# Preparing two stages' weights and first chunks inside the feed-forward loops ahead of them, with the on-chip memory laid out anew

## The chip, the cores and the metric

The kernel runs on one core of one Trainium2 chip. The metric is the device time of one execution in microseconds (us), the median of the runs. TensorE (PE in the profile) multiplies matrices, PEld is its loading of stationary operands, VectorE (DVE), ScalarE (ACT) and GpSimd (POOL) work on elements, and SyncE (SP) issues the DMAs. On-chip memory is 128 partitions wide; the matmul results go to eight banks of 512 numbers per partition (`PS[0]` to `PS[7]`).

## The reference

Six stages follow one another over 8192 rows of 256 numbers (8 sequences of 1024), each reading the layer norm of the running sum `x`:

```python
x = x + 0.5 * L0_ffn(layernorm(x))    # stage S=0: first feed-forward
x = x +       L0_attn(layernorm(x))   # stage S=1: first attention
x = x + 0.5 * L0_ffn(layernorm(x))    # stage S=2
x = x + 0.5 * L1_ffn(layernorm(x))    # stage S=3: second feed-forward
x = x +       L1_attn(layernorm(x))   # stage S=4: second attention
x = x + 0.5 * L1_ffn(layernorm(x))    # stage S=5

# L0_ffn: blocks of 16 numbers quantized to FP4 and back, on activations and weights
def fp4_linear(x, w): return einsum('bsk,nk->bsn', fp4(x), fp4(w))
h = silu(fp4_linear(x, w_gate)) * fp4_linear(x, w_up)     # 704 wide
out = fp4_linear(h, w_down)

# L0_attn: 16 heads of 16, one decaying state per head
qkv = x @ Wqkv.T + b;  k = k / 4;  g = sigmoid(gamma_raw)
state = g * state + outer(v_t, k_t);  y_t = state @ q_t   # over 1024 steps
out = y @ out_w.T + out_b

# L1_ffn: ternary weights
scale = max(mean(abs(w)), 1e-8);  w_t = clip(round(w / scale), -1, 1)
out = gelu(x @ w1_t.T + b1) @ w2_t.T + b2                 # 1024 wide
```

## The kernel before

All of `x` stays on chip as 64 tiles `X[:, n, :]` of 128 rows; four tiles make a chunk, 16 chunks a stage (`NS`), 64 tiles a stage (`NT`). Every engine's program is one list written out by hand and carried out in order; engines wait for one another only by semaphores. Nothing reorders the work, so the order of the lines is the order of the queues.

Each stage needs three things before its first matmul. (1) Its weights and tables. (2) Chunk 0 normalised: VectorE takes the statistics (`stats`, L181), GpSimd makes the factors (`spread`, L200), ScalarE applies them (`norm`, L212) into `XN`. (3) Chunk 0 turned: TensorE transposes `XN` into a bank (`turn_pe`, L231), ScalarE copies the high part to `XTH` (`turn_act`) and VectorE the rest to `XTL` (`low_dve`).

The loops `ffn0_pe`, `ffn0_act`, `ffn0_dve`, `ffn0_pool` run over tile `n` (chunk `i = n // 4`, place in it `j = n % 4`) and are pipelined over several tiles: in its turn `n` TensorE makes the down-product of tile `n-4` (L575), at `j` 2 and 3 a transposition of half of chunk `i+1` (L233), the up-products of tile `n` in three parts (L46 to L48), between them the transposition of tile `n-3` (L590). VectorE's turn holds two halves of the FP4 rounding (L274, L277), the update of `X` (L643), work on the chunks `i+1` and `i+2`, and the product `fH` of tile `n` (L664) with its block scales. Those on chunks stop at the stage's last chunk (`if i + 1 < NS`).

When such a loop ends, `ffn0_end` (L704) makes every engine wait until the stage is over. Then comes the preparation of the next: `attn0_set_sp`, `_act`, `_dve`, `_pe`, `_pool` for the first attention (weights split in a high and a low part, powers of the decay made on VectorE, written to HBM and read back in shifted form as `hankel`, two matmuls with `rev` at L829 and L830 and their copies to `DT` and `KD`), `ffn1_set_sp`, `_dve`, `_pe` for the second feed-forward (mean of the absolute weights, then the ternary masks at L1185 and L1187, 2048 numbers at a time for each of two matrices). `attn0_ready` and `ffn1_ready` are the waits on it. After them every engine prepares chunk 0 of the stage, and only then comes the first projection (L46) or up-product (L1312). Memory is shared: the attention's buffers start where those of stage 0's loop do, and the buffers of the second feed-forward and attention start at the address of all that came before them.

## Time and profile before

| | us |
|---|---|
| median of 3 runs (2841.96 to 2848.13) | 2843.5 |
| the profiled execution | 2847.05 |
| its span, first to last instruction | 2844.9 |
| TensorE busy | 2573.6 (90%) |
| VectorE busy | 1784.6 (63%) |
| ScalarE busy | 1374.1 (48%) |
| GpSimd busy | 1141.7 (40%) |

The busy shares are averages over stages that differ. A stretch in which TensorE is busy for the whole of its length is bound by TensorE; one in which it stands still shows in its idle time, written in square brackets in a timeline, with the engine or the DMA that ended it. The granted clock is 1.00 at 2.4 GHz and 0.50 at 1.2 GHz. L-numbers are lines of the kernel before.

### The profile page before, as it was taken

To read this page: it belongs to the slowest core of one execution; us is meant where nothing else is said; L and a number is where in the kernel's file an instruction comes from. 1 tells how busy PE (TensorE), PEld (TensorE's weight loads), DVE (VectorE), ACT (ScalarE), POOL (GpSimd) and SP (SyncE) were. 2 spreads that over 40 slices of the span, in tenths; PEclk is the share of its full clock that TensorE was granted. 3 is DMA by queue.
4 is the path that set the end of the run, shared out by engine and by line. 5 is a ranking of instruction groups with operands and counts; after the bars stand their busy time and mean duration, and the time that the engine had idled before them with its cause. 6 is when DMAs were issued, how large, how long until landed. Compare 5 with 4: busy or idle time off the path is not lost.

```text
span 2844.9 us, 75949 instructions
## 1 busy us (share of the span) xinstructions
PE 2573.6 (90%) x31466; PEld 2155.5 (76%) x31466; DVE 1784.6 (63%) x4172; ACT 1374.1 (48%) x2283; POOL 1141.7 (40%) x1382
## 2 busy tenths in 40 slices
PE   4999999678989969999999499989999999979998
PEld 3888888567777757888887388877788888858887
DVE  7878887445555548788785466554556666545554
ACT  3444444234444424444443477765445444417776
POOL 5555555233333325555553233311444444353332
PEclk8999999889999989999999799999999999979999
DMA  4000000100001100000000100000000000000001
GB/s 151 1 1 1 1 1 1 25 13 22 21 21 22 22 16 1 1 1 1 1 1 1 47 1 1 1 5 18 18 17 17 16 18 16 19 3 23 31 30 38
DMA packets 67557, 45.85 MB, mean 16 GB/s; under 512 B 13184, under 2 KB 66192, under 8 KB 67216
## 3 DMA queue, kind: packets, MB, share of 16 engines
q1 hardware_dynamic: 67216, 41.00, 5.2%
q8 instruction: 251, 4.11, 0.6%
q14 instruction: 90, 0.74, 0.1%
HBM read 15.78 MB, written 8.40 MB: 9 GB/s over the span
## 4 chain that ended last, share of the span: by engine, by line
PE 27%; issue 13%; POOL 11%; DVE 6%; ACT 6%; DMA 0%; SPq 0%; POOLq 0%; ACTq 0%; DVEq 0%
PE ps L575 6%; PE ps L46 3%; PE ps L48 3%; PE ps L47 3%; ACT XN L221 2%; PE ps L233 2%; PE ps L1312 2%; POOL rs L206 2%; DVE st L190 2%; POOL a1pry L1887 2%; POOL a1pry L1889 2%; PE ps L1313 2%; ACT gHf L1353 2%; POOL a1l L1875 2%; DVE XTL L243 1%
## 5 line engine op out<-in xcount | busy, mean ns | idle before, releaser
L575 PE MATMUL ps<-WDT,fHT 128*128 128x256 f32 (+1 forms) x1536 | 379.7, 389 | 8.5 <-ACT fHT L615 8.5
L1382 DVE TENSOR_TENSOR gHl<-gHf,gHh 128x512 fp32r<-128x512 f32 x256 | 180.6, 706 | 254.3 <-ACT gHh L1357 254.2
L575 PEld LDWEIGHTS ps<-WDT,fHT 128*128 128x128 f32 (+1 forms) x1536 | 279.3, 190 | 80.1 <-issue 42.5
L687 POOL TENSOR_TENSOR fV<-fH,frc 128x704 f32<-128x704 f32 x128 | 178.3, 1393 | 356.9 <-DVE frc L676 356.9
L46 PE MATMUL ps<-WGH,XTH 128*128 128x512 f32 (+1 forms) x768 | 314.1, 409 | 3.2 <-DVE XTL L243 1.4
L48 PE MATMUL ps<-WGL,XTH 128*128 128x512 f32 (+1 forms) x768 | 290.2, 378 | 0.0
L47 PE MATMUL ps<-WGH,XTL 128*128 128x512 f32 (+1 forms) x768 | 290.0, 378 | 0.0
L1327 PE MATMUL ps<-W2T,gHh 128*128 128x256 f32 x1024 | 256.1, 283 | 0.0
L1329 PE MATMUL ps<-W2T,gHl 128*128 128x256 f32 x1024 | 253.7, 281 | 0.0
L221 ACT ACTIVATE XN<-X,nb,rs 128x256 f32<-128x256 f32 x384 | 198.9, 589 | 98.3 <-POOL nb L210 98.3
L664 DVE TENSOR_TENSOR fH<-ps,fSG 128x704 f32<-128x704 f32 x128 | 113.9, 890 | 194.6 <-ACT fSG L621 183.2
L609 ACT ACTIVATE ps<-fV 128x704 fp32r<-128x704 f32 x128 | 97.5, 762 | 281.2 <-DVE fV L277 273.5
L1312 PE MATMUL ps<-XTH,W1T 128*128 128x512 f32 x512 | 208.8, 408 | 19.6 <-DVE XTL L243 18.3
L1353 ACT ACTIVATE gHf<-ps,B 128x512 f32<-128x512 f32 x256 | 175.2, 684 | 99.8 <-PE ps L1313 99.7
L239 ACT ACTIVATE XTH<-ps 128x512 fp32r<-128x512 f32 x192 | 108.0, 594 | 215.4 <-PE ps L233 215.3
L694 POOL TENSOR_TENSOR fHX<-fV,fsc 128x704 f32<-128x704 f32 x128 | 178.2, 1392 | 69.9 <-DVE fV L277 69.9
L1313 PE MATMUL ps<-XTL,W1T 128*128 128x512 f32 x512 | 204.9, 400 | 0.0
L204 POOL TENSOR_SCALAR ve<-mv 128x4 f32<-128x4 f32 x96 | 32.9, 342 | 426.3 <-DVE mv L196 422.5
L1329 PEld LDWEIGHTS ps<-W2T,gHl 128*128 128x128 f32 x1024 | 193.5, 189 | 10.2
L1327 PEld LDWEIGHTS ps<-W2T,gHh 128*128 128x128 f32 x1024 | 192.8, 188 | 9.6
L1875 POOL TENSOR_TENSOR a1l<-a1l,a1rc 128x128 f32<-128x128 f32 x128 | 49.7, 410 | 363.0 <-DVE a1rc L1842 363.0
L46 PEld LDWEIGHTS ps<-WGH,XTH 128*128 128x128 f32 x768 | 146.4, 191 | 42.5 <-issue 21.2
(227 smaller groups left out, 6395.8 us busy)
## 6 DMA issues: line engine op xcount, KB each, us to landing
X<-in_x SPq DMA_DIRECT2D x16, 512.0 KB, 8.9
a0vp<-a0vt SPq DMA_DIRECT2D x256, 32.0 KB, 1.9
a1vp<-a1vk SPq DMA_DIRECT2D x256, 32.0 KB, 2.2
out<-X SPq DMA_DIRECT2D x16, 512.0 KB, 2.9
tws<-in_w SPq DMA_DIRECT2D x2, 1024.0 KB, 7.8
WN<-in_wgu SPq DMA_DIRECT2D x3, 384.0 KB, 5.0
a0km<-in_wqkv SPq DMA_DIRECT2D x2, 384.0 KB, 3.4
a1pry<-in_aw SPq DMA_DIRECT2D x1, 768.0 KB, 4.5
```

The source lines that it names most:

```text
L46: e.matmul(o, hh, mh, start=first, stop=False)
L47: e.matmul(o, hl, mh, start=False, stop=False)
L48: return e.matmul(o, hh, ml, start=False, stop=last)
L221: t = act.activation(XN[:, j, :], X[:, 4 * i + j, :], ACT.Identity, scale=rs[b][:, j:j + 1], bias=nb[b][:, j:j + 1])
L575: h = pe.matmul(down, HT[n % 2][0:m, c, :], WDT[0:m, c, :], start=(c == 0), stop=(c == 5))
L687: pool.tensor_tensor(s3(V[(n - 1) % 2][:, :]), s3(H[(n - 1) % 2][:, :]), cast16(rc[(n - 1) % 2][:, :], 44), ALU.mult).then_inc(s_hv, 1)
L1312: pe.matmul(PS[m % 2][:, :], W1T[:, k, fs], XTH[b][:, k, :], start=(k == 0), stop=False)
L1313: t = pe.matmul(PS[m % 2][:, :], W1T[:, k, fs], XTL[b][:, k, :], start=False, stop=(k == 1))
L1327: pe.matmul(o, Hh[w][:, js], W2T[:, f, :], start=(f == 0 and j % 2 == 0), stop=False, skip_group_check=True)
L1329: t = pe.matmul(o, Hl[w][:, js], W2T[:, f, :], start=False, stop=(f == 7), skip_group_check=True)
L1353: act.activation(Hf[u][:, :], PS[m % 2][:, :], ACT.Gelu, bias=B1[:, f:f + 1]).then_inc(s_ge, 1)
L1382: dve.tensor_tensor(Hl[m % 8][:, :], Hf[m % 4][:, :], Hh[m % 8][:, :].bitcast(F32), ALU.subtract).then_inc(s_hl, 1)
```

## The change

The preparation of the first attention moves into the loop of stage 0, and that of the second feed-forward into the loop of stage 2. `attn0_set_dve` becomes eight steps at the turns `n` = 10 to 17 of stage 0, `ffn1_set_dve` nineteen steps at the turns 8 to 17, 22, 24 to 31 and 33 of stage 2. `attn0_set_act` runs at turns 8, 9, 34 and 38 and `attn0_set_pe` at 34 and 38 of stage 0, `ffn1_set_pe` at 22 of stage 2. These products use the bank `PS[3]`, which also holds the turned chunks, so TensorE waits there until the bank has been read: `pe.wait_ge(s_dte, n + 1)` and `pe.wait_ge(s_tern, 4)`. The two exponentials of the preparation stand in front of stage 0's loop, and the DMAs of the tables behind those of `x` in SP's list. The DMAs of the ternary matrices are issued when the first attention has ended.

The loop no longer stops at the last chunk: statistics, factors, normalisation, transposition and both copies of the next stage's chunk 0 are done in its last turns. `ffn0_end` goes; `ffn0_banks` and later waits on the last update of `X` stand where banks or memory are reused. In the attention, VectorE takes chunk 1's statistics first. For all this the preparation needs memory of its own: the second half's weights start at 15960 numbers per partition behind the shared tiles, and the masks are made 512 numbers at a time.

```diff
-        lay1 = top.enter_context(ExitStack())
-        W1T = sb(lay1, "W1T", [P, 2, FF], R32)
-        W2T = sb(lay1, "W2T", [P, 8, D], R32)
...
+        sb(lay1, "over", [P, 15960])
+        W1T = sb(lay1, "W1T", [P, 2, FF], R32)
...
         def x_turn_pe(pe, S, i, k):
             F = 16 * S + i
-            pe.wait_ge(s_qxx, 8 * S + i + 1)
+            if i < NS:
+                pe.wait_ge(s_qxx, 8 * S + i + 1)
+            else:
+                pe.wait_ge(s_xn, F + 1)
             if F or k:
                 pe.wait_ge(s_xl, 2 * F + k)
-            turn_pe(pe, F, k, PS[3], XV)
+            turn_pe(pe, F, k, PS[3], XV if i < NS else xf)
...
                     h.then_inc(s_dn, 1)
-                if n < NT and j in (2, 3) and i + 1 < NS:
+                if n == 34 and S == 0:
+                    pe.wait_ge(s_qxx, i + 2)
+                    attn0_set_pe(pe, 0)
+                if n == 38 and S == 0:
+                    pe.wait_ge(s_qxx, i + 2)
+                    attn0_set_pe(pe, 1)
+                if n == 22 and S == 2:
+                    pe.wait_ge(s_qxx, 16 + i + 2)
+                    ffn1_set_pe(pe)
+                if n < NT and j in (2, 3):
                     x_turn_pe(pe, S, i + 1, j - 2)
                 if n < NT:
                     if j == 0:
...
                 t = tb + n
                 i, j = n // 4, n % 4
-                if n < NT and j in (2, 3) and i + 1 < NS:
+                if n in (34, 38) and S == 0:
+                    attn0_set_act(act, 2 + (n - 34) // 4)
...
+                if n == NT - 4:
+                    norm(act, S + 1, 0)
+                if n in (8, 9) and S == 0:
+                    attn0_set_act(act, n - 8)
...
+                if n in when0 and S == 0:
+                    attn0_set_dve(dve, when0.index(n))
+                if n in when1 and S == 2:
+                    ffn1_set_dve(dve, when1.index(n))
+                if n < NT and j < 2 and i + 1 < NS:
+                    x_grid(dve, S, i + 1, j)
+                if n < NT and j > 1:
+                    x_low(dve, S, i + 1, j - 2)
+                if n < NT and j < 3 and i + 2 <= NS:
+                    for k in ((0, 1), (2, 3), (4, 5, 6, 7))[j]:
+                        stats(dve, *chunk(16 * S + i + 2), k)
...
-        def ffn0_end(e, S):
-
-            e.wait_ge(s_dn, 32 * S + NT)
-            e.wait_ge(s_he, 32 * S + NT)
-            e.wait_ge(s_hx, 32 * S + NT)
-            e.wait_ge(s_xd, 64 * S + NT)
...
+        def ffn0_banks(pe, S):
+
+            pe.wait_ge(s_hm, 32 * S + NT)
+            pe.wait_ge(s_hq2, 32 * S + NT)
...
         def attn0_set_sp(sp):
...
-            ffn0_end(sp, 0)
-            for k in range(2):
-                sp.dma_start(KM[k][:, :, :].rearrange("p k t -> p (k t)")[:, 0:768],
-                             wqkv[128 * k:128 * k + 128, :]).then_inc(d_wqkv, 16)
...
+            sp.wait_ge(s_wt, 12)
+            for k in range(2):
+                sp.dma_start(KM[0][:, k, 0:768], wqkv[128 * k:128 * k + 128, :]).then_inc(d_wqkv, 16)
...
+        def attn0_set_exp(act):
+            act.wait_ge(d_gam, 16)
             act.activation(g1[:, 1:2], g1[:, 0:1], ACT.Exp, scale=-1.0).then_inc(s_ga, 1)
...
+        def attn0_set_act(act, n):
+
+            if n < 2:
+                act.wait_ge(d_wqkv, 32)
+                act.activation(a0WH[:, n, :], KM[0][:, n, 0:768], ACT.Copy).then_inc(s_a0h, 1)
...
+        def attn0_set_dve(dve, n):
+
+            if n < 2:
+                dve.wait_ge(s_a0h, n + 1)
+                dve.tensor_tensor(a0WL[:, n, :], KM[0][:, n, 0:768], a0WH[:, n, :].bitcast(F32),
+                                  ALU.subtract).then_inc(s_a0l, 1)
...
+        def attn0_set_pe(pe, n):
+
             pe.wait_ge(d_hank, 96)
-            pe.wait_ge(d_a0, 96)
-            pe.matmul(PS[0][:, :], rev[:, :], hankel[:, 0:512], start=True, stop=True).then_inc(s_dt, 1)
-            pe.matmul(PS[1][:, 0:64], rev[:, :], hankel[:, 512:576], start=True, stop=True).then_inc(s_dt, 1)
+            pe.wait_ge(d_a0, 80)
+            src = hankel[:, 0:512] if n == 0 else hankel[:, 512:576]
+            pe.matmul(PS[3][:, 0:512 if n == 0 else 64], rev[:, :], src, start=True, stop=True).then_inc(s_dt, 1)
...
         def attn0_set_pool(pool):
-            ffn0_end(pool, 0)
...
@@ -946,7 +989,7 @@
                             if k == 1 and q == 3:
                                 t.then_inc(s_up, 1)
 
-            turn_x(0)
+            ffn0_banks(pe, 0)
             proj(0, (0, 1))
...
+                    pe.wait_ge(s_xd, NT)
                 if 0 <= m < NT:
...
-            norm(act, 1, 0)
-            turn_x(0)
             proj(0, (0, 1))
             proj(0, (2, 3))
             norm(act, 1, 1)
+            act.wait_ge(s_dn, NT)
...
-            low(0)
+                stats(dve, 1, 1, k)
             late(0)
-            for k in range(8):
-                stats(dve, 1, 1, k)
...
-            ffn0_end(sp, 2)
...
+        def ffn1_set_dve(dve, step):
+
+            if step < 8:
+                n, c = divmod(step, 4)
+                if c == 0:
+                    dve.wait_ge(d_w[n], 16)
+                t = dve.tensor_reduce(tam[n][:, 16 * c:16 * c + 16],
+                                      tws[n][:, 512 * c:512 * c + 512].rearrange("p (a b) -> p a b", b=32), AX, ALU.add,
+                                      apply_absolute_value=True)
+                if c == 3:
...
+                n, c = divmod(step - 10, 4)
+                cs = slice(512 * c, 512 * c + 512)
+                v, a = tws[n][:, cs], ta[c % 2]
+                dst = (W1T, W2T)[n][:, :, :].rearrange("p k n -> p (k n)")[:, cs]
+                dve.wait_ge(s_tern, 5 + 2 * (step - 10))
+                dve.tensor_scalar(a[:, :], v, ta1[n][:, 3:4], None, ALU.is_lt).then_inc(s_tern, 1)
+                dve.wait_ge(s_tern, 6 + 2 * (step - 10))
+                dve.scalar_tensor_tensor(out=dst, in0=v, scalar=ta1[n][:, 2:3], in1=a[:, :], op0=ALU.is_gt,
                                          op1=ALU.subtract).then_inc(s_tern, 1)
-            dve.wait_ge(d_b1, 32)
...
         def ffn1_set_pe(pe):
-            ffn0_end(pe, 2)
-            for n in range(2):
-                pe.wait_ge(s_tern, 6 * n + 2)
-                pe.matmul(PS[n][:, 0:1], ones[:, :], ta1[n][:, 0:1], start=True, stop=True).then_inc(s_ternp, 1)
+
+            pe.wait_ge(s_tern, 3)
...
         def ffn1_ready(e):
 
-            e.wait_ge(s_tern, 13)
+            e.wait_ge(s_tern, 22)
...
             if S == 3:
-                turn_x(0)
+                ffn0_banks(pe, 2)
             for m in range(8 * NS + LAG):
                 i, f = m // 8, m % 8
+                if S == 3 and m == LAG:
+                    pe.wait_ge(s_xd, 64 * 2 + NT)
...
             if S == 3:
-                norm(act, 3, 0)
-                turn_x(0)
+                act.wait_ge(s_dn, 64 + NT)
...
-            if S == 3:
-                for k in range(8):
-                    stats(dve, 3, 0, k)
-                low(0)
...
+            attn0_set_exp(act)
             ffn0_act(act, 0)
-            attn0_set_act(act)
             attn0_ready(act)
...
             ffn1_act(act, 3)
...
             start_dve(dve)
             ffn0_dve(dve, 0)
-            attn0_set_dve(dve)
             attn0_ready(dve)
...
             ffn1_ready(dve)
...
```

TensorE's list where the first attention opens (L575/L591 down-products, L590/L615 transpositions of the last tiles, a0wh the attention's weights), before:

```order
L590 MATMUL ps<-ident,fHX 64x128
L575 MATMUL ps<-WDT,fHT 128x256 x6
L829 MATMUL ps<-a0qp,a0rev 128x512
L830 MATMUL ps<-a0qp,a0rev 128x64
L233 MATMUL ps<-ident,XN 128x128 x8
L46 MATMUL ps<-XTH,a0wh 128x512
```

and now:

```order
L591 MATMUL ps<-WDT,fHT 128x256 x6
L615 MATMUL ps<-ident,fHX 128x128 x5
L615 MATMUL ps<-ident,fHX 64x128
L591 MATMUL ps<-WDT,fHT 128x256 x6
L46 MATMUL ps<-XTH,a0wh 128x512
```

The two products with `a0rev` and the eight transpositions of `XN` no longer stand between the last down-product and the first projection.

TensorE's list at the start of turn 34 of the first stage (the rows end with the turned chunk's transposition and the first up-products), before:

```order
L47 MATMUL ps<-WGH,XTL 128x384
L48 MATMUL ps<-WGL,XTH 128x384
L575 MATMUL ps<-WDT,fHT 128x256 x6
L233 MATMUL ps<-ident,fXV 128x128 x4
L46 MATMUL ps<-WGH,XTH 128x512
```

and now:

```order
L47 MATMUL ps<-WGH,XTL 128x384
L48 MATMUL ps<-WGL,XTH 128x384
L591 MATMUL ps<-WDT,fHT 128x256 x6
L871 MATMUL ps<-a0qp,a0rev 128x512
L246 MATMUL ps<-ident,fXV 128x128 x4
L46 MATMUL ps<-WGH,XTH 128x512
```

One product with `a0rev` has come in between the down-product and the transpositions; its 64-column fellow stands in the same place four turns later.

ScalarE's list in front of stage 0's loop (fXV the chunk's FP4 values, a0g and a1g the two tables of exponentials), before:

```order
L480 ACTIVATE WDT<-ps 64x256
L309 ACTIVATE ps<-fXV 128x512
L621 ACT_TABLE_LOAD
L621 ACTIVATE fSG<-ps 128x704
L309 ACTIVATE ps<-fXV 128x512
```

and now:

```order
L496 ACTIVATE WDT<-ps 64x256
L322 ACTIVATE ps<-fXV 128x512
L813 ACTIVATE a0g<-a0g 16x1
L815 ACTIVATE a1g<-a1g 128x16
L648 ACT_TABLE_LOAD
L648 ACTIVATE fSG<-ps 128x704
```

The exponentials have come in front of the table load; the load that stood before them in the first gap and the one at the opening of stage 2 are gone from ScalarE's list.

## Rows read from the trace of the kernel before

**Rows 1.** The page: granted clock of TensorE, tenths of full speed, 40 slices of 71.1 us.

```profile
PEclk8999999889999989999999799999999999979999
```

**Rows 2.** Stretches around both stage changes: length, engines' busy us, clock, DMA share, GB/s.

```profile
495.00:530.00 35.00, 35.00 (x172) 28.48 (x170) 19.46 (x38) 10.99 (x15) 12.16 (x9) 1.00 0.00 1
530.00:549.50 19.50, 13.92 (x56) 9.53 (x56) 4.87 (x10) 3.11 (x4) 4.16 (x3) 0.91 0.00 0
549.50:581.60 32.10, 4.30 (x12) 2.74 (x12) 7.93 (x31) 7.10 (x13) 5.71 (x12) 0.58 0.24 55
1553.00:1570.50 17.50, 11.93 (x56) 8.16 (x54) 4.50 (x9) 3.11 (x4) 4.16 (x3) 1.00 0.00 0
1570.50:1603.50 33.00, 3.09 (x13) 2.58 (x13) 16.71 (x26) 4.03 (x7) 6.48 (x24) 0.57 0.32 102
```

**Rows 3.** Timeline of TensorE at the first change: start, us, engine, line [idle<-releaser].

```profile
546.37 3.05 PE L575 MATMUL ps<-WDT,fHT 128*128 128x256 f32 x12 [0.90 <-ACT fHT L615]
568.56 2.04 PE L829 MATMUL ps<-a0qp,a0rev 128*128 128x512 f32 x2 [19.14 <-DMA a0GQ<-pw_scratch]
570.40 0.53 PE L830 MATMUL ps<-a0qp,a0rev 128*128 128x64 f32 x2
...
581.66 0.80 PE L46 MATMUL ps<-XTH,a0wh 128*128 128x512 f32 x1 [1.41 <-DVE XTL L243]
```

**Rows 4.** Timeline of the other engines in the first gap.

```profile
555.36 1.83 DVE L800 TENSOR_TENSOR a0wl<-a0km,a0wh 128x768 fp32r<-128x768 f32 x2 [5.48 <-ACT a0wh L786]
...
570.96 0.60 ACT L793 ACTIVATE a0DT<-ps 128x512 f32<-128x512 f32 x1 [13.38 <-PE ps L830]
```

**Rows 5.** Timeline of TensorE at the second change.

```profile
1567.39 3.05 PE L575 MATMUL ps<-WDT,fHT 128*128 128x256 f32 x12 [0.90 <-ACT fHT L615]
...
1603.50 0.79 PE L1312 MATMUL ps<-XTH,W1T 128*128 128x512 f32 x1 [1.41 <-DVE XTL L243]
```

**Rows 6.** Timeline of VectorE in the second gap.

```profile
1582.34 1.29 DVE L1185 TENSOR_SCALAR ta<-tws,ta 128x2048 f32<-128x2048 f32 x1
1583.66 2.35 DVE L1187 SCALAR_TENSOR_TENSOR W1T<-tws,ta 128x2048 fp32r<-128x2048 f32 x1
```

**Rows 7.** Timeline of TensorE inside the first feed-forward loop, tiles two to four.

```profile
152.57 2.95 PE L575 MATMUL ps<-WDT,fHT 128*128 128x256 f32 x12
...
160.44 2.95 PE L575 MATMUL ps<-WDT,fHT 128*128 128x256 f32 x12
...
167.90 2.95 PE L575 MATMUL ps<-WDT,fHT 128*128 128x256 f32 x12
```

**Rows 8.** VectorE's waits from 90 to 520 us: us in total, times, longest.

```profile
DVE fH L664 <- ACT fSG L621: 81.1, 54, 3.1
```

**Rows 9.** Timeline of VectorE inside the same loop.

```profile
156.33 0.88 DVE L277 SCALAR_TENSOR_TENSOR fV<-ps,fV 128x704 f32<-128x704 f32 x1
...
160.69 0.89 DVE L664 TENSOR_TENSOR fH<-ps,fSG 128x704 f32<-128x704 f32 x1 [0.70 <-ACT fSG L621]
```

**Rows 10.** Timeline of the DMA issues and ScalarE at the start.

```profile
6.03 20.94 SPq L259 DMA_DIRECT2D X<-in_x  x15
...
43.80 1.28 ACT L621 ACT_TABLE_LOAD   x1
48.82 0.76 ACT L621 ACTIVATE fSG<-ps 128x704 f32<-128x704 f32 x1 [3.74 <-PE ps L48]
```

**Rows 11.** Short stretches that open the first attention and the second feed-forward kind.

```profile
581.60:590.00 8.40, 8.01 (x30) 6.46 (x30) 3.19 (x11) 3.74 (x6) 0.35 (x2) 0.79 0.00 0
1603.50:1610.00 6.50, 6.50 (x17) 5.06 (x18) 2.96 (x10) 4.10 (x7) 0.50 (x1) 0.57 0.00 0
```

**Rows 12.** Timeline of ScalarE, VectorE and TensorE where the third stage opens.

```profile
1070.68 1.28 ACT L621 ACT_TABLE_LOAD   x1
...
1072.77 0.89 DVE L664 TENSOR_TENSOR fH<-ps,fSG 128x704 f32<-128x704 f32 x1
...
1072.79 0.50 PE L46 MATMUL ps<-WGH,XTH 128*128 128x512 f32 x1 [1.03 <-ACT fSG L621]
```

More of the change, by code:

```diff
@@ L72, in macaron @@
         WDT = sb(lay0, "WDT", [P, 6, D])
+        XV = sb(lay0, "fXV", [P, 4 * D])
+        xsc = [sb(lay0, f"fxsc{i}", [P, 64]) for i in range(2)]
+        xsn = sb(lay0, "fxsn", [P, 64])
+        xrc = sb(lay0, "fxrc", [P, 64])
         f0 = ExitStack()
-        XV = sb(f0, "fXV", [P, 4 * D])
-        xsc = [sb(f0, f"fxsc{i}", [P, 64]) for i in range(2)]
-        xsn = sb(f0, "fxsn", [P, 64])
-        xrc = sb(f0, "fxrc", [P, 64])
         SG = [sb(f0, f"fSG{i}", [P, NF]) for i in range(2)]
@@ L91, in macaron @@
         a0 = ExitStack()
+        QTb = sb(a0, "a0qt1", [P, 2, 512])
+        KMb = sb(a0, "a0km1", [P, 2, 1024])
+        KTb = sb(a0, "a0kt1", [P, 2, 512])
+        QPb = sb(a0, "a0qp1", [P, 2, 512])
+        a0A = [sb(a0, f"a0A{i}", [P, 1024]) for i in range(2)]
+        VK = [sb(a0, f"a0vk{i}", [P, 512]) for i in range(2)]
+        QT = [sb(a0, "a0qt0", [P, 2, 512]), QTb]
+        KM = [sb(a0, "a0km0", [P, 2, 1024]), KMb]
+        KT = [sb(a0, "a0kt0", [P, 2, 512]), KTb]
+        QP = [sb(a0, "a0qp0", [P, 2, 512]), QPb]
         a0WH = sb(a0, "a0wh", [P, 2, 768], R32)
@@ L728, in slots0 @@
         def slots0():
-            yield from [("t", 0, 0), ("t", 0, 1), *[("p", 0, o) for o in range(4)]]
+            yield from [("p", 0, o) for o in range(4)]
             for n in range(NT + 2):
@@ L1121, in attn0_pool @@
             attn0_ready(pool)
-            spread(pool, 1, 0)
             add_bias(pool, 1, 0, bot[:, :], 0)
@@ L1199, in ffn1_ready @@
+            pe.matmul(PS[3][:, 0:2], ones[:, :], tsum[:, :], start=True, stop=True).then_inc(s_ternp, 1)
+            pe.wait_ge(s_tern, 4)
         def ffn1_ready(e):
[L1201 removed]
+            e.wait_ge(s_tern, 22)
         a1WS = PRY[:, :].rearrange("p (k n) -> p k n", k=2)
```

218 lines of the change are left out of this document (103 added, 115 removed).

## The prediction

> **What bounds the kernel.** I read the clock's line on the page first [rows 1]. It is at 9 tenths nearly everywhere and dips only in a few of the 40 slices; two of the dips, in the eighth and in the twenty-third slice, are where a feed-forward loop hands over. Then the busy times by stretch [rows 2]. From 495 to 530 us TensorE is busy for 35.00 of 35.00 us: the loop is bound by TensorE, and anything that makes its list longer there is paid in full. From 530 to 549.5 us the loop runs dry (13.92 of 19.50 us). Then follow 32.10 us in which TensorE is busy for 4.30, and at the second change 33.00 us with 3.09. There the bound is the preparation: a chain over all engines in which the matrix engine has nothing to do. Last come the timelines, which give the edges of both gaps and the prices of what is moved.
>
> First gap: the last down-product starts at 546.37 and takes 3.05, so it ends at 549.42; the first projection starts at 581.66 [rows 3]. That is 32.24 us. Inside, TensorE waits 19.14 us for a DMA, the last link of a chain of table work and small transfers, then makes the two products with the reversed identity, then waits for ScalarE's copy [rows 3, 4], the statistics, the normalisation and the turning of chunk 0. Second gap: from 1567.39 + 3.05 = 1570.44 to 1603.50, 33.06 us [rows 5].
>
> **What goes.** Nothing of the preparation stands between the last down-product and the first product of the next stage any more; the list of TensorE shows them side by side. What is left to wait for there is VectorE's last product and rounding of the loop, which feed the very down-products that stand ahead, and so are over. I leave 0.1 us for a hand-over in each: 32.1 + 33.0 = 65.1 us. The drain before it (from 530 to 549.5 us, and from 1553 to 1570.5) stays as it is: the same instructions follow one another there, and its own waits are not touched.
>
> **What the opening of the stages gains besides.** After the gap TensorE is at its lower level. From 581.6 to 590 us the granted clock is 0.79, from 1603.5 to 1610 it is 0.57 [rows 11]. With levels 1.0 and 0.5 these are 3.5 us and 5.6 us at 1.2 GHz, and what was done in them would take half at 2.4 GHz: 1.8 and 2.8 us. In the drains before the gaps the clock is 0.91 and 1.00 [rows 2], so the projections should now start near the higher level. How much of that reaches the end depends on the others. In the attention ScalarE works through the four projections and then normalises chunk 1, each behind TensorE's results; I take 1.3 us, with 0 and 1.8 as the ends. In the second feed-forward ScalarE's Gelu and copies are the slower part after two products, and GpSimd now clears its buffers in the same time in which it used to wait; I take 0.4 us, between 0 and 2.8. Together 1.7 us.
>
> The Trainium skill (TensorE: Matmul & The Clock Gate, section Part 1: The HAM clock gate) says that the lower rate is the default and that activity releases it. By this rule a stage that follows without a gap starts at the higher rate, and the sum gets up to the 4.6 us named; if the drain counts as idleness it gets nothing. The clock at the drains' ends [rows 2] speaks for the first.
>
> **What is added to TensorE's list.** The loop is bound by TensorE, so these count in full.
> - Four transpositions of half a chunk, two in each of the two loops. Their price is the difference between turns with one and without: from 152.57 to 160.44 is 7.87 us, from 160.44 to 167.90 is 7.46 [rows 7]. So 0.41 us each, 1.6 us in all. They were in the gap before.
> - The two products with the reversed identity, at turns 34 and 38, and the wait until ScalarE has copied the bank. The first took 570.40 - 568.56 = 1.84 us at the lower level [rows 3], so 0.9 at the higher; the copy takes 0.60 [rows 4], and two hand-overs 0.1. The wait is new: behind it in TensorE's list stand the transposition of the next chunk and the up-products of the tile, and the whole loop waits for those. 1.6 us. The second took 0.53, so 0.3, and its copy is of 16 columns: 0.5 us in all. Together 2.1 us, between 1.3 (if the copies cost nothing) and 3.6 (lower level, and half a microsecond of hand-overs).
> - The product for the mean at turn 22 of the third stage. TensorE waits for VectorE to scale it, and VectorE does so only after its rounding step. In such a turn the down-product ends at 152.57 + 2.95 = 155.52 and the rounding at 156.33 + 0.88 = 157.21 [rows 7, 9]; with two short operations and a hand-over of 0.3 us together TensorE goes on at 157.5. So 2.0 us, between 0.3 (if VectorE is early) and 2.9 (if it also has to catch up by one operation of its own, 0.9).
>
> Sum of the added: 1.6 + 2.1 + 2.0 = 5.7 us.
>
> **What I cost at nothing, and its cover.** VectorE gets the work of both gaps, at most 7.93 + 16.71 = 24.6 us busy [rows 2], spread over 8 turns of the first stage and 19 of the third. It has waits to put it in: 54 times, 81.1 us in total between 90 and 520 us [rows 8], 1.50 us a turn. The heaviest steps are the eight of the masks: a comparison of 1.29 / 4 and a second of 2.35 / 4 [rows 6], 0.91 us a turn. The shortest wait of the four turns of a chunk is 0.70 [rows 9], so there `fH` comes 0.2 us late. That does not reach TensorE: `fH` ends at 160.69 + 0.89 = 161.58, and TensorE needs it for the second up-product, after a down-product that lasts from 160.44 to 163.39, so at least 1.8 us later. The high and low halves of the attention's weights, 1.83 us for two [rows 4], fall into turns 10 and 11 in the same way.
> ScalarE's exponentials in front of the loop wait for a small DMA that is issued behind those of `x`. These issues end at 6.03 + 20.94 = 26.97 us, and ScalarE gets there at 43.80; the activation that follows starts only at 48.82 after 3.74 us of waiting [rows 10]. Two small operations would have to use up those 3.74 us before they cost anything.
> The tables come from HBM long before their use: VectorE's last step on them is at turn 17, TensorE's first use at turn 34, seventeen turns of 7.5 us later.
> One table load goes at the opening of the third stage: 1.28 us, and TensorE's second tile waited for what followed it, 1.03 us [rows 12]. But VectorE started `fH` at 1072.77 straight behind its own work, without idle time [rows 12], so the next link does not come earlier; I take 0, at most 1.0. The Trainium skill (ScalarE: Activation LUTs, section What ACT_TABLE_LOAD costs) gives a load about 2.7 us; by that the term would be up to 2.4 us. The trace has 1.28 us, and that decides.
>
> **The sum.** 65.1 + 1.7 - 5.7 = 61.1 us. The profiled execution took 2847.05 us (its span and 2.15 us around it), so 2785.9 us. It was 3.55 us above the median of 2843.5 us; against the median the forecast is 2782 us.
>
> **Rivals.**
> 1. VectorE's added work does not fit. Its waits are averages, the semaphores between two steps on the same data cost time of their own, and in the turns of the masks the waits are nearly used up. For it: 0.91 against 0.70 us. Against it: 1.50 on average and the 1.8 us before TensorE notices. If half of the 24.6 us shows up, the gain is 12.3 us smaller: 2794 us.
> 2. The stages are joined but a start-up wait takes the gap's place: the attention's first tile needs chunk 1's bias and the copies in a fixed order on GpSimd and ScalarE, and these now begin when the loop has drained. For it: the stretch from 581.6 to 590 us has GpSimd at 0.35 us busy [rows 11], so it waits for others there too. If each stage start lost 4 us more than before: 2790 us.
> 3. The change does not do what it says, one table coming too late so that TensorE stands inside the loop. For the attention that would need a delay of seventeen turns, 127 us. I see nothing that could do it; if it were the third stage's masks, the wait would be the part of the 33 us that is not done, up to 2815 us.
> 4. Slower than before: with both rests gone the clock is lowered in the stages behind them. TensorE would then need about twice the time for the same work; from 61 us of such work on, the gain is lost, and if the first 100 us after each change ran at 1.2 GHz, the time would be 2782 + 200, some 2980 us. Against it: 9 tenths of the clock over hundreds of microseconds of a fully busy engine [rows 1, 2].
>
> **How the numbers follow.** The forecast has 0.80, rival 1 0.10, rival 2 0.07, rivals 3 and 4 0.015 each. The forecast's own range comes from the ends of the terms: gains up to 65.3 + 1.8 + 2.8 + 1.0 with the least additions (1.4 + 1.3 + 0.3) give 67.9 us, 2776; no gain from the clock and the largest additions (1.6 + 3.6 + 2.9) give 57 us, 2786.5. The runs before lie 1.5 us below and 4.6 above their median, which I add in part, and the upper side takes in rivals 1 and 2: 2774 to 2795 us. About 0.2% can be told from no change here, 5.7 us. Faster by more than that: all but rival 4 and a residue, 0.98; the same 0.01; slower 0.01.
>
> **What would show it.** In the profile after, the first projection should follow the last down-product within 0.5 us, and the first up-product of the fourth stage likewise. The clock's line should lose its two dips. At turns 34 and 38 of the first stage TensorE should stand for 0.6 to 0.8 and 0.2 us behind ScalarE, at turn 22 of the third for about 1.7 us behind VectorE. VectorE's waits in the changed turns should shrink but stay above nothing, and TensorE should show no wait for `fH` or for its scales there. ScalarE should load five tables instead of seven. The prediction is wrong if TensorE waits inside the loops anywhere else, or if over 5 us of idle time are left at either change.

## The result

| | time, us | ratio to the kernel before, 95% interval |
|---|---|---|
| before | 2842.7, median of 4 runs (2841.1 to 2848.1) | |
| changed kernel | 2794.4, median of 4 (2790.8 to 2801.7) | 0.983 (0.9805 to 0.9855) |
| the same, second comparison | 2789.3, median of 4 (2783.7 to 2796.1), against 2844.3 | 0.9807 (0.9788 to 0.9826) |

The forecast was 2782 us in a range of 2774 to 2795, faster with 0.98. The change gains 48 and 55 us in the two comparisons where 61 were forecast. The eight runs together have a median of 2791.5, 9.5 us above the forecast.

The page of the changed kernel, with its span and the line of the granted clock that answers to [rows 1]:

```profile
span 2790.3 us, 75964 instructions
PEclk9999999899999989999999999999999999989999
```

TensorE's timeline at the two changes, where [rows 3, 5] had 32 and 33 us (columns: start, us, engine, line, operation, in brackets the idle time before it and who ended it):

```profile
551.17 4.71 PE L591 MATMUL ps<-WDT,fHT 128*128 128x256 f32 x12 [0.90 <-ACT fHT L642]
555.81 0.50 PE L46 MATMUL ps<-XTH,a0wh 128*128 128x512 f32 x1
...
1548.02 3.05 PE L591 MATMUL ps<-WDT,fHT 128*128 128x256 f32 x12 [0.90 <-ACT fHT L642]
1551.00 0.50 PE L1373 MATMUL ps<-XTH,W1T 128*128 128x512 f32 x1
```

The first product of the next stage begins as the last down-product ends. The granted clock over the drains and openings (columns as in [rows 2]; the third row has the attention's first waits, the last the fourth stage behind its own):

```profile
528.79:555.81 27.02, 21.52 (x67) 14.82 (x66) 6.86 (x12) 3.11 (x4) 6.89 (x7) 0.68 0.00 1
555.81:563.81 8.00, 6.49 (x31) 5.28 (x30) 3.62 (x11) 4.92 (x8) 1.71 (x4) 1.00 0.00 0
563.81:575.81 12.00, 7.69 (x118) 6.88 (x122) 3.57 (x10) 4.63 (x9) 4.66 (x7) 0.57 0.06 12
1529.20:1551.00 21.80, 16.29 (x68) 11.38 (x66) 6.86 (x12) 3.11 (x4) 4.16 (x3) 0.92 0.00 0
1563.00:1567.00 4.00, 4.00 (x16) 3.61 (x15) 1.48 (x2) 3.60 (x7) 3.20 (x4) 0.50 0.01 4
```

The projections run at full clock (1.00, where [rows 11] had 0.79), but the clock falls some 9 us later, behind the first of two waits for the attention's keys, and in the fourth stage behind the wait for chunk 1. Of the page's two dips the second is gone (7 in the twenty-third slice before); the first, 88 before, is still an 8 in the eighth slice, where the drain lies.

TensorE's waits in the two loops, from 60 to 540 us and from 1060 to 1530 us (us in total, times, longest):

```profile
PE ps L591 <- ACT fHT L642: 2.6, 2, 1.4
PE ps L615 <- DVE X L674: 1.7, 3, 1.0
PE ps L246 <- ACT a0DT L824: 0.7, 1, 0.7
PE ps L246 <- ACT a0KD L827: 0.3, 1, 0.3
```

```profile
PE ps L615 <- DVE X L674: 3.7, 6, 1.0
PE ps L246 <- DVE ta L1229: 1.6, 1, 1.6
PE ps L591 <- ACT fHT L642: 1.0, 1, 1.0
PE ps L246 <- POOL fXV L335: 0.3, 2, 0.2
```

The waits behind `a0DT`, `a0KD` and `ta` were forecast. The six for VectorE's residual `X` were not: the text said that TensorE would wait nowhere else in the loops. They stand in the turns of the masks. By the prediction's own sign ("wrong if TensorE waits inside the loops anywhere else") this part of it failed.

**Where the time went**, by TensorE's edges: starts of down-products (numbered by turn), of the first product of a stage, and the end. The turn numbered n in what follows is the time from the down-product of turn n-1 to that of turn n, so the products that the code makes behind the down-product of turn 34 show at turn 35.

| stretch | before | after | gain |
|---|---|---|---|
| start to turn 4 of the first loop | 68.04 | 64.84 | 3.2 |
| first loop, turns 4 to 64 | 459.61 | 463.95 | -4.3 |
| turn 64 to the first projection (drain and gap) | 54.01 | 27.02 | 27.0 |
| attention and opening of the third stage | 509.02 | 505.75 | 3.3 |
| third loop, turns 4 to 64 | 459.61 | 467.68 | -8.1 |
| turn 64 to the first up-product (drain and gap) | 53.21 | 21.76 | 31.5 |
| rest | 1241.40 | 1239.30 | 2.1 |
| span | 2844.9 | 2790.3 | 54.6 |

Turn by turn the two loops agree to 0.02 us except where the change put work. In the first: 0.32 at turn 5, 0.65 at turns 18 and 19 (the powers of the decay), 1.82 at turn 35, 0.70 at turn 39, 0.78 at the last two. In the third: 1.95 at turn 23, 5.35 over turns 26 to 33, 0.79 at the last two. A second trace of the changed kernel repeats each of these to 0.03 us, but for the 0.32: a difference of that size at turn 5 is in some traces of either kernel and not in others.

### The profile page after: what moved, and what is told of

It reads as the page before. It is cut to its first block, busy times and chain, and to the rows that moved or that the text cites. A ratio compares the mean times of both kernels' runs of the same rounds, so it can differ in the third digit from the quotient of the medians.

```text
span 2790.3 us, 75964 instructions
## 1 busy us (share of the span) xinstructions
PE 2565.9 (92%) x31464; PEld 2148.2 (77%) x31464; DVE 1795.8 (64%) x4190; ACT 1369.6 (49%) x2281; POOL 1146.1 (41%) x1382
## 4 chain that ended last, share of the span: by engine, by line
PE 25%; issue 13%; POOL 11%; DVE 8%; ACT 6%; SPq 0%; DMA 0%; POOLq 0%; DVEq 0%; ACTq 0%
PE ps L591 5%; PE ps L46 3%; PE ps L48 3%; PE ps L47 3%; PE ps L246 2%; PE ps L1373 2%; ACT XN L234 2%; DVE st L203 2%; POOL rs L219 2%; PE ps L1374 2%; POOL a1pry L1943 2%; POOL a1pry L1945 2%; POOL a1l L1931 2%; ACT gHf L1413 2%; DVE XTL L256 1%
## 5 line engine op out<-in xcount | busy, mean ns | idle before, releaser
L591 PE MATMUL ps<-WDT,fHT 128*128 128x256 f32 (+1 forms) x1536 | 386.0, 394 | 8.7 <-ACT fHT L642 8.7
L591 PEld LDWEIGHTS ps<-WDT,fHT 128*128 128x128 f32 (+1 forms) x1536 | 283.4, 192 | 82.4 <-issue 42.8
L727 POOL TENSOR_TENSOR fHX<-fV,fsc 128x704 f32<-128x704 f32 x128 | 180.9, 1413 | 71.1 <-DVE fV L290 71.1
```

The lines of the kernel that those rows point to most:

```text
L591: h = pe.matmul(down, HT[n % 2][0:m, c, :], WDT[0:m, c, :], start=(c == 0), stop=(c == 5))
L727: pool.tensor_tensor(s3(HX[n % 2][:, :]), s3(V[n % 2][:, :]), cast16(sc[(n - 2) % 3][:, :], 44), ALU.mult).then_inc(s_hx, 1)
```

## The experiments

**1. The changed kernel again, and the drains.**

> The changed kernel once more, for a second trace and a firmer gain. Theory A (the instruction stream sets the waits): the turns of the three loops repeat to 0.05 us, the mask turns of the third stage cost 5.3 us again, and only the drains of the two loops differ, because the clock there falls or does not: the first drain between 22 and 27 us, the second between 17 and 22. Theory B (the first profile was an odd run): the mask turns cost something else, or the drain of the first stage is 21.8 us as before. Time 2790 to 2800 us in both, 45 to 53 us below the kernel before.

Measured: 2789.3 us (above), 55.1 below the kernel before, a little outside the 45 to 53 named. The turns are as in the first trace and the mask turns cost 5.3 us: theory A for the loops. From turn 64 to the next stage it took 27.21 and 21.76 us, nearly what the first trace had, so this run does not show that the drains vary; they needed a test of their own.

**2. The drains filled.** In front of each wait of the drain TensorE transposes the identity into a bank that is free.

```diff
+            def filler(count):
+                pe.wait_ge(s_xl, 2 * (16 * S + 16) + 2)
+                for _ in range(count):
+                    pe.transpose(PS[3][:, 0:128], ident[:, :], ident[:, :])
...
                 if 4 <= n < NT + 4:
                     q = t - 4
+                    if n > NT:
+                        filler(10)
                     pe.wait_ge(s_he, q + 1)
...
                 if 3 <= n < NT + 3:
                     q = t - 3
+                    if n >= NT:
+                        filler(5)
                     pe.wait_ge(s_hx, q + 1)
```

> Only change: TensorE fills its waits in the drains of the two loops with transpositions of the identity into a bank that is free (ten ahead of each wait for the halves, five ahead of each wait for the last products), so that it does not idle there. Theory A (the drain of the first stage took 27.0 us where it had taken 21.8 because the clock fell in its idle stretches): the granted clock stays at 1.0 through both drains, the down-products there take 3.05 us and the drains 20 to 22 and 15 to 17 us; 4 to 7 us below the changed kernel, and its runs lie closer together. Rival B (the drain is bound by the chain over ScalarE, GpSimd and VectorE, and the clock only colours it): the drains stay within 1 us of those of the changed kernel, or get longer by what the fillers delay.

Measured: 2778.6 us (2776.7 to 2781.7), 10.7 us below the changed kernel on the same chip, ratio to the kernel before 0.9772 (0.9758 to 0.9787). The same down-products of the first drain, first in the changed kernel, then filled:

```profile
535.08 5.78 PE L591 MATMUL ps<-WDT,fHT 128*128 128x256 f32 x12 [1.44 <-ACT fHT L642]
543.88 4.94 PE L591 MATMUL ps<-WDT,fHT 128*128 128x256 f32 x12 [0.90 <-ACT fHT L642]
```

```profile
537.32 3.05 PE L598 MATMUL ps<-WDT,fHT 128*128 128x256 f32 x12 [0.35 <-ACT fHT L651]
540.30 0.76 PE L586 MATMUL ps<-ident 128*128 128x128 f32 x5
540.98 0.85 PE L624 MATMUL ps<-ident,fHX 128*128 128x128 f32 x6
541.66 1.25 PE L586 MATMUL ps<-ident 128*128 128x128 f32 x10
542.76 3.02 PE L598 MATMUL ps<-WDT,fHT 128*128 128x256 f32 x12
```

Both drains take 20.1 us, at clock 1.00, as they do in the two kernels below that fill them (20.08 to 20.10). The second was expected at 15 to 17 us, so that part of the expectation was wrong. Without fillers the eleven drains with no gap behind them, in six traces of the changed kernel and its variants, took 27.02, 27.21, 27.17, 27.24, 20.07, 25.09 (first) and 21.76, 21.76, 25.09, 25.10, 23.43 us (second). Theory A holds: with waits of 0.9 to 1.4 us between short pieces of work the clock fell in ten of these eleven drains, and then up to three down-products took 4.7 to 5.8 us each; with the waits filled it fell in none of six. The time fell by more than the 4 to 7 us named: first drain 7.1 us, second 1.7, and the attention with the opening behind it, which no filler touches, took 497.3 us against 502.1. That last part can't be told from chance: the attention varies by as much among kernels that have the same one.

**3. Does the kernel before do that as well?** Two more traces of it.

> The kernel before once more, for a second trace of it. Open is whether its drains and its attention vary as those of the changed kernel do. Theory A (the clock falls in the drains or not, by chance of its phase, in both kernels): drain and gap together, from the down-product of turn 64 to the first product of the next stage, are not 54.0 and 53.2 us again but differ by 1 to 7 us, while the turns of the loops repeat to 0.05 us. Rival B (the drains of the kernel before are always at full clock, and the changed kernel slows them): 54.0 and 53.2 us again to 0.5 us.

> As the one ahead of it, a third trace of the kernel before: by theory A the two sums differ from one trace to the next by 1 to 7 us, by rival B they stay at 54.0 and 53.2 us to 0.5 us.

Measured: 2855.4 and 2849.1 us; drain and gap together 59.43 and 60.12 us, then 54.25 and 60.27, against 54.01 and 53.21 in the first trace. The last down-product of each drain splits these sums: the gaps alone are 32.24, 32.20, 32.72 us and 33.06, 32.93, 33.06 us, and the drains 21.77, 27.23, 21.53 us and 20.15, 27.19, 27.21 us. In the first of the two new traces the drain looked so:

```profile
533.05 5.79 PE L575 MATMUL ps<-WDT,fHT 128*128 128x256 f32 x12 [1.44 <-ACT fHT L615]
541.87 5.04 PE L575 MATMUL ps<-WDT,fHT 128*128 128x256 f32 x12 [0.90 <-ACT fHT L615]
549.26 4.74 PE L575 MATMUL ps<-WDT,fHT 128*128 128x256 f32 x12 [0.90 <-ACT fHT L615]
```

Theory A: three of the four new sums differ by 5.4 to 7.1 us from the first trace, one by 0.2. The drains of the kernel before vary as those of the changed one do, and nothing shows that the change slows them; the trace on which the forecast rested happened to have two nearly undisturbed ones. Over the three traces of before, drain and gap take 55.9 and 57.9 us on average, without gap 25.6 and 23.4 (the eleven above). The difference is 64.7 us, and 65.1 were forecast. With drains that vary by 7 us and three traces on one side, such an average is good to a few us; the gaps alone are known to half a microsecond.

**4. The masks at another place in the turn.**

```diff
-                if n in when1 and S == 2:
+                if n in when1 and S == 2 and when1.index(n) < 10:
                     ffn1_set_dve(dve, when1.index(n))
...
                 if n < NT and j == 3 and i + 2 < NS:
                     x_scale(dve, S, i + 2)
+                if n in when1 and S == 2 and when1.index(n) >= 10:
+                    ffn1_set_dve(dve, when1.index(n))
                 if n < NT:
                     dve.wait_ge(s_sg, t + 1)
```

> Only change: the eight mask steps (and the last step on the bias) stand at another place in VectorE's turn of the third stage, in front of fH and no longer right behind the sums that also release GpSimd's product fHX. Theory A (the second mask operation stands beside GpSimd's product and shares its way to SBUF): it falls from 1.76 us to 0.6 to 0.8, GpSimd's product beside it from 1.57 to 1.39, and the turns 25 to 33 cost under 1.5 us together where they cost 5.35, so 3.5 to 4.5 us less in all. Rival B (VectorE's turn is simply too full, however the work is placed): the operation stays near 1.7 us and the turns cost 5 us or more. Rival C: it is fast there, but fH and what follows come late by its 0.9 us in the turns with the shortest wait, and TensorE loses 2 to 4 us of the gain again.

Measured: 2789.0 us (2784.0 to 2794.5), the changed kernel's 2789.3 on the same chip. The mask turns cost 4.4 us together, 0.9 less. What happens shows in the timelines of VectorE and GpSimd. First the changed kernel, a mask beside GpSimd's product:

```profile
1221.80 0.48 DVE L1242 TENSOR_SCALAR ta<-tws,ta 128x512 f32<-128x512 f32 x1
1221.97 1.56 POOL L727 TENSOR_TENSOR fHX<-fV,fsc 128x704 f32<-128x704 f32 x1 [0.48 <-DVE fV L290]
1222.32 1.76 DVE L1244 SCALAR_TENSOR_TENSOR W1T<-tws,ta 128x512 fp32r<-128x512 f32 x1
```

Then the moved masks, in four turns:

```profile
1237.48 1.39 POOL L729 TENSOR_TENSOR fHX<-fV,fsc 128x704 f32<-128x704 f32 x1 [0.48 <-DVE fV L290]
1238.20 0.95 DVE L1244 TENSOR_SCALAR ta<-tws,ta 128x512 f32<-128x512 f32 x1
...
1247.39 2.02 POOL L315 TENSOR_TENSOR fXV<-XN,fxrc 128x1024 f32<-128x1024 f32 x1 [1.39 <-DVE fxrc L308]
1247.66 2.31 DVE L1246 SCALAR_TENSOR_TENSOR W1T<-tws,ta 128x512 fp32r<-128x512 f32 x1
...
1253.61 0.85 PE L615 MATMUL ps<-ident,fHX 128*128 128x128 f32 x6 [1.33 <-DVE X L674]
...
1256.67 0.75 DVE L1246 SCALAR_TENSOR_TENSOR W2T<-tws,ta 128x512 fp32r<-128x512 f32 x1
...
1263.15 1.94 POOL L335 TENSOR_TENSOR fXV<-fXV,fxsc 128x1024 f32<-128x1024 f32 x1
...
1263.62 1.75 DVE L1244 TENSOR_SCALAR ta<-tws,ta 128x512 f32<-128x512 f32 x1
```

Alone the second operation takes 0.75 us and the first 0.48 (eight of each in experiment 6's gap). In the changed kernel GpSimd's product ends at 1221.97 + 1.56 = 1223.53, and the mask at 1224.08, 0.55 later; in the next case GpSimd ends at 1249.41 and the mask at 1249.97, 0.56 later; in the last at 1265.09 and the first operation at 1265.37, 0.28 later. The same first operation that began later in a product of GpSimd (1238.20) took only 0.95 us and ended 0.28 after it too. So the VectorE instruction stands until GpSimd's has ended and then does nearly all of its work, 0.2 us less than it takes alone. It is no sharing: one waits for the other's end, and the product of GpSimd that had begun first took its usual time (`fXV` at L335: 1.93 to 1.95 us in all 32). The Trainium skill (SBUF — State Buffer, section Who interferes with whom) says just that: an operation of VectorE with two inputs in SBUF, or in a mode that uses both ports, and a GpSimd operation that reads SBUF exclude each other, and the one that issues second is blocked until the first has ended. The rows agree. Theory A's mechanism is right, as far as one excludes the other, and its forecast of the gain wrong; the time is nearest to rival C. The late place meets GpSimd's other products in six of the eight turns (1.75, 0.95 and 2.31 us for one operation, each twice). `fH`, which stands behind the mask, and `X` behind that then come late, and TensorE waits for `X` four times, 0.34 to 1.33 us. The two turns in which the masks meet nothing cost nothing.

**5. The masks in the turns that have room.** One in each chunk, at the same place in the turn as in the changed kernel.

```diff
-        when1 = (*range(8, 16), 17, 22, *range(24, 32), 33)
+        when1 = (*range(8, 16), 17, 22, *range(26, 58, 4), 59)
```

> Only change: the eight mask steps and the last one on the bias stand in the turns 26, 30, 34 ... 54 and 59 of the third stage, one in each chunk, where VectorE waits 2.6 us for its next Silu; their place within the turn is that of the changed kernel, right behind the sums that release GpSimd's product. Theory A (the second mask operation stands still until GpSimd's product beside it has ended, and this costs only where VectorE has less than that to spare): the operation still takes 1.76 us, but the turns 25 to 33 lose their 5.35 us and the eight new places cost under 0.2 us each; 4 to 5.4 us less in the loop. Rival B (1.76 us in a turn reach TensorE wherever they stand): about 0.65 us in each of eight turns, 5 us again, no gain. In the time 2784 to 2788 us by A, 2789 to 2793 by B.

Measured: 2786.5 us (2784.4 to 2795.1), 0.9803 of the kernel before (0.9773 to 0.9832); the time alone doesn't tell it from the changed kernel. The loop does: the 5.35 us are gone to 0.02 us, no new turn costs 0.02 us, and TensorE's waits for `X` have left the list. The operation is as slow as it was:

```profile
1227.36 1.57 POOL L727 TENSOR_TENSOR fHX<-fV,fsc 128x704 f32<-128x704 f32 x1 [0.48 <-DVE fV L290]
1227.71 1.76 DVE L1244 SCALAR_TENSOR_TENSOR W1T<-tws,ta 128x512 fp32r<-128x512 f32 x1
...
1230.75 0.89 DVE L697 TENSOR_TENSOR fH<-ps,fSG 128x704 f32<-128x704 f32 x1 [0.40 <-ACT fSG L648]
```

In such a turn of the kernel before, VectorE waits 2.60 us at the same place:

```profile
152.82 0.89 DVE L664 TENSOR_TENSOR fH<-ps,fSG 128x704 f32<-128x704 f32 x1 [2.60 <-ACT fSG L621]
```

Theory A: the mask's 0.48 + 1.76 us fit into the 2.60 and leave 0.40. A blocked operation costs where VectorE has less to spare than the block.

**6. The weights prepared in the gap again.** The 19 steps and TensorE's mean product go back behind the third loop; chunk 0 stays inside it.

```diff
-                if n in when1 and S == 2:
-                    ffn1_set_dve(dve, when1.index(n))
...
+            for step in range(19):
+                ffn1_set_dve(dve, step)
```

> The scaling of the fourth stage's weights, its masks and the mean product are done behind the third stage's loop again (VectorE's 19 steps and TensorE's product), while chunk 0 is still normalised and turned inside the loop and the DMAs stay early. Theory A (moving VectorE's steps pays their whole duration in the gap and costs the loop the 1.95 us of turn 22 and the 5.35 of the mask turns): the loop of the third stage gets 7.3 us shorter, a gap of 15 to 19 us opens between it and the first up-product, and the fourth stage opens cold; in all 9 to 14 us slower than the changed kernel. Rival B (the gap was bound by chunk 0's chain over ScalarE and GpSimd, so the weights alone lie beside it): the gap stays under 8 us and the time within 3 us of the changed kernel, or below it.

Measured: 2797.5 us (2793.9 to 2812.0), 8.2 above the changed kernel on the same chip. The loop is free of the 1.95 and the 5.35 us, and the gap is back:

```profile
1544.30 4.74 PE L591 MATMUL ps<-WDT,fHT 128*128 128x256 f32 x12 [0.90 <-ACT fHT L639]
...
1566.67 0.77 PE L1368 MATMUL ps<-XTH,W1T 128*128 128x512 f32 x1 [11.41 <-DVE B L1243]
```

17.6 us lie between. Theory A, a little under its 9 to 14 us (the traced execution, 2812.0 us, was the longest of the four by 13 us, so its parts outside the loop and the gap say little): VectorE's list alone was half of the second gap. Moving it was worth 17.6 us less the 7.3 that it costs in the loop, and less what falls to chance.

**7. Products ahead of the down-product.** The two products with `rev` and the mean product go in front of the turn's down-product, so that the reader has 2.95 us for its part, and TensorE's waits for the reader go behind it; the powers of the decay are made one in a turn.

```diff
+                if n in (35, 39) and S == 0:
+                    pe.wait_ge(s_xl, 2 * (16 * S + i + 1) + 1)
+                    attn0_set_pe(pe, (n - 35) // 4)
+                if n == 23 and S == 2:
+                    pe.wait_ge(s_xl, 2 * (16 * S + i + 1) + 1)
+                    ffn1_set_pe(pe)
                 if 4 <= n < NT + 4:
...
+                if n == 35 and S == 0:
+                    pe.wait_ge(s_dte, 1)
+                if n == 39 and S == 0:
+                    pe.wait_ge(s_dte, 2)
+                if n == 23 and S == 2:
+                    pe.wait_ge(s_tern, 4)
...
-        when0 = (10, 11, 12, 13, 14, 15, 16, 17)
+        when0 = (10, 11, 12, 13, 14, 15, 16, 17, 18, 19, 20, 21, 22)
```

> Changed: the two products with the reversed identity (turns 35 and 39 of the first stage) and the product of the mean (turn 23 of the third) stand in front of the turn's down-product, so that their readers copy or scale beside those 2.95 us, and the powers of the decay are made one in a turn. Theory A (what these places cost, 1.82, 0.70 and 1.95 us, is nearly all TensorE waiting for a reader, and the 0.65 of the powers is VectorE beside GpSimd): the three places cost only their products, 0.4 to 0.9, 0.1 to 0.3 and 0.3 to 0.5 us, the powers under 0.2; 3.5 to 4 us less, and the clock does not fall behind turn 23, which it did in two of four profiles for another 1.6 us. Rival B (the wait only moves: the product now holds up the down-product, or its reader comes late): 2 us or more remain at the first and the third place, and the gain is under 2 us. Time 2783 to 2788 us by A, 2788 to 2792 by B.

Measured: 2782.5 us (2782.1 to 2783.8), 0.9784 (0.9757 to 0.981). Turn 35 costs 0.87 us where it cost 1.82, turn 39 0.17 for 0.70, turn 23 0.20 for 1.95, the powers nothing for 0.65. Over the two loops it is 3.8 us less, as theory A has it. TensorE behind the mean product in the changed kernel, and behind the same wait in the kernel with filled drains:

```profile
1202.42 0.38 PE L1253 MATMUL ps<-tsum,ones 128*128 128x2 f32 x2
1204.38 0.66 PE L246 MATMUL ps<-ident,fXV 128*128 128x128 f32 x4 [1.57 <-DVE ta L1229]
1205.11 0.39 PE L47 MATMUL ps<-WGH,XTL 128*128 128x512 f32 x1
```

```profile
1191.29 1.06 PE L246 MATMUL ps<-ident,fXV 128*128 128x128 f32 x4 [1.57 <-DVE ta L1238]
1192.57 0.63 PE L47 MATMUL ps<-WGH,XTL 128*128 128x512 f32 x1
```

The same wait of 1.57 us in a loop that is otherwise full left the clock alone in three traces of five and lowered it in two (experiments 2 and 4), for another 1.6 us.

**8. All three edits** (2, 5 and 7):

> Three edits together on the changed kernel: the drains filled, the products put ahead with the powers one in a turn, the masks in the turns where VectorE has 2.6 us to spare. If the costs are separate, as theory A has them, their gains add: about 10 us (drains and the clock behind them), 5.3 (masks), 4 to 5 (products), so 2768 to 2772 us against 2789 of the changed kernel. Rival B (the run-to-run part, the clock's falls in the attention, takes a share back): 2773 to 2779 us.

Measured: 2767.9 us (2765.9 to 2773.5), 0.9735 (0.9707 to 0.9763). The gains add, as by theory A (2768 to 2772 expected): the loops take 461.9 and 461.0 us, each drain 20.08. This is the fastest version: 77.7 us below the kernel before on the same chip, 23.6 below the changed kernel's median of eight.

**9. The openings filled too.** 14 and 30 transpositions in the attention's first tile, 34 in front of chunk 1 in the fourth stage; the attention's wait for the last `X` moves ahead of the first ones. The second of the three places:

```diff
                 if n == 0:
-                    pe.wait_ge(s_xd, NT)
+                    for _ in range(30):
+                        pe.transpose(PS[7][:, 0:128], ident[:, :], ident[:, :])
```

> As the kernel with all three edits, and TensorE's waits at the openings are filled as well: 14 and 30 transpositions of the identity in the attention's first tile (waits of 1.97 and 3.86 us) and 34 in the fourth stage in front of the turning of chunk 1 (4.45 us). Theory A (the granted clock of 0.50 to 0.62 from 563.8 to 575.8 us and from 1563 to 1567 us follows from those waits, and what runs in it takes twice the time on the way that sets the end): the clock stays at 1.0 in both places and 3 to 6 us go, 2764 to 2767 us. Rival B (there ScalarE, VectorE and GpSimd set the pace, TensorE's clock matters little): under 1.5 us.

Measured: 2775.1 us (2768.6 to 2778.8). The clock does what was asked, for the stretch of 4 us in the wait for the keys, first without and then with fillers:

```profile
560.42:564.42 4.00, 1.49 (x37) 1.45 (x38) 0.77 (x4) 0.00 (x0) 2.41 (x4) 0.50 0.07 16
```

```profile
561.75:565.75 4.00, 2.83 (x55) 2.49 (x53) 0.77 (x4) 0.42 (x1) 2.44 (x4) 1.00 0.07 16
```

At the wait for chunk 1 the fillers held it at 1.00 over 4 us too, where it was 0.70. But nothing comes earlier for it. From the first projection to the first growth of the state it is 14.49 us where it was 14.51, from the fourth stage's first up-product to the turning of chunk 1 it is 11.45 where it was 11.44, and the attention to the third stage's first up-product takes 478.9 us where it took 477.6. Rival B: there the other engines set the pace. The median is 7 us higher, which neither theory has; the ranges overlap, and what of it is more than chance is open.

## Why the forecast was nearly right

- **The gaps, 65.1 us: right.** The gaps alone are 65.1 to 65.8 us in the three traces of before and nothing afterwards; with the drains the averages give 64.7.
- **"The drain before it stays as it is": wrong as a statement on one execution**, and on average not refuted (23.5 and 24.9 us in three traces before, 25.6 and 23.4 after). The drains vary from 20.1 to 27.2 us in both kernels. The forecast had taken its time from a trace with good drains, whose time was still 3.55 us above the median: a median of runs and the parts of one trace don't belong together to a few us.
- **Opening of the stages, 1.7 us: too low.** The attention with the opening behind it took 509.0, 508.1 and 506.6 us before and 497.3 to 505.8 (mean 501.8, nine traces of the changed kernel and its variants) without the gap: 6 us, not 1.3. 1.6 to 2.8 of them lie in the opening: from first projection to the first growth of the state 597.80 - 581.66 = 16.14 us before (16.47 and 17.27 in its other traces), 570.38 - 555.81 = 14.57 after (14.52). Where the rest comes from is open; the clock's falls in the attention differ from trace to trace. The rest of the program had 0.4 for its opening and shows none (1239.7 on average before, 1239.6 after).
- **Four transpositions, 1.6 us: right** (0.78 + 0.79).
- **The two products with `rev`, 2.1 us: 2.5.** The first wait was 0.69 us as named, but its product took 1.12 us and not 0.9.
- **The mean product, 2.0 us: right** (1.95); the wait of 1.57 was named as 1.7. That such a wait can lower the clock was not seen.
- **VectorE's work at nothing: this is the step that failed.** 5.35 us for the masks, 0.65 for the powers. The cover was argued with 0.91 us of work against 0.70 of waiting. The price was divided by width from one long instruction (2.35 / 4 = 0.59 in [rows 6]), while four short ones take 0.75 each (and the first operation 0.48, not 1.29 / 4 = 0.32), and it was read in a gap, where GpSimd had nothing to do. Beside GpSimd's product it is 1.76. So a mask turn adds 0.48 + 1.76 = 2.2 us to VectorE, three times the shortest wait. The text looked for the delay at `fH`, 1.8 us ahead of its reader; it came out one step further, at `X`, behind which the transposition of `HX` stands. Rival 1 had this place right and 12.3 us as its price; it was half of that.
- **The table load at 0: right**; ScalarE has five loads where it had seven, and from the third stage's first up-product to turn 4 it is 24.1 to 24.8 us in the three traces of before and 24.0 to 24.9 in those after.
- **Start-up waits (rival 2): there, and small.** ScalarE and TensorE where the fourth stage opens:

```profile
1552.30 1.28 ACT L1413 ACT_TABLE_LOAD   x1 [4.33 <-PE ps L1374]
...
1554.34 0.50 PE L1373 MATMUL ps<-XTH,W1T 128*128 128x512 f32 x1 [1.21 <-ACT gHf L1413]
...
1562.46 1.97 PE L246 MATMUL ps<-ident,XN 128*128 128x128 f32 x8 [4.45 <-ACT XN L234]
```

  The load for Gelu, which lay in the gap, now stands behind the first product, and TensorE waits 1.21 us for it; chunk 1 keeps it waiting 4.45 us where it had 3.01, 3.92 and 3.95 in the three traces of before. Together 1.7 to 2.7 us, against 4 for each stage start in rival 2. The attention's start shows nothing of the kind.

In sum, trace against trace the change gained 54.6 us where 61.1 were forecast. The two loops cost 12.4 us where 5.7 were named, and drain and gap gave 58.5 us for 65.1, because the drains of this pair of traces went against the change. Against these 13 us stand 3.7 more than named from the stages and their openings, and 3.2 at the start of the program, which nobody forecast. That the time fell into the range owes something to these parts cancelling.

Averages of traces do not close with the medians. The three traces of before are of executions of 2847.1, 2855.4 and 2849.1 us, above all its medians (2842.7 to 2845.6), so their averages credit the change with 59.5 us, where the medians have 48 and 55. A term that is an average over these traces, the 6 us of the attention above all, is uncertain by as much. Only what repeats is firm: the gaps, and the 12 us of the loops.

## What to carry to other kernels

Price a moved instruction where it will stand, not where it stood: look who else runs in that microsecond. Here the mask operations of VectorE waited out each product of GpSimd that had begun before them, so such work belongs in a turn that has the whole of that wait to spare; another place in the same full turn met other products and gave back 0.9 us of 5.35. A wait of TensorE behind a product that it had just made for another engine went away when the product moved in front of the next long one.

## What the runs showed of the hardware

- An empty stretch need not be long to cost clock: in drains with 0.9 to 1.4 us waits between pieces of 0.85 and 3 us, the granted clock fell to 0.68 on average in one trace and stayed at 1.00 in another with the same instructions in its drain (experiment 5). Twenty us of such work varied by 7 us. Idle transpositions, 0.8 and 1.25 us at a time, ended that (six of six drains took 20.1 us).
- Behind a single wait of 1.57 us in an otherwise full loop the clock fell in two traces of five.
- A full clock gave nothing where other engines set the pace: 14.49 against 14.51 us and 11.45 against 11.44 us in two openings.
- VectorE and GpSimd excluded each other for whole instructions: 0.75 us of work took 1.76 and 2.31, 0.48 took 1.75, and in all 38 cases in five traces it ended 0.27 to 0.56 us after GpSimd's product. GpSimd's 1.39 became 1.56 where VectorE had begun first.
